# Earlier first exponentials of a softmax attention, fed by their own quad's maxima, and unread products among the row maxima

## The reference, cut to what matters

```python
c_q = x @ W_dq;  Q = (c_q @ W_uq).reshape(Bx, Sx, 16, 8)
c_kv = x @ W_dkv
K = (c_kv @ W_uk).reshape(Bx, Sx, 16, 8)
V = (c_kv @ W_uv).reshape(Bx, Sx, 16, 8)
scores = jnp.einsum('bqhd,bkhd->bhqk', Q, K) / math.sqrt(8)
scores = jnp.where(causal, scores, -jnp.inf)
attn = jax.nn.softmax(scores, axis=-1)
out = jnp.einsum('bhqk,bkhd->bqhd', attn, V).reshape(Bx, Sx, 128)
return out @ W_o
```

## Time and profile before

| | |
|---|---|
| median of 3 runs | 1094.41 us (1093.99 to 1094.48) |
| the profiled execution's own time | 1092.62 us |
| its span, first to last instruction | 1090.8 us |
| TensorE busy | 963.0 us, 88% |
| VectorE busy | 756.0 us, 69% |
| mean granted TensorE clock | 0.923 of 2.4 GHz |

### The profile page before, as it was taken

The page is one execution under the profiler, slowest core; times in us unless marked ns, Lnnn a source line. Parts: engine busy times, 40 slices in busy tenths (PEclk is TensorE's granted clock), DMA queues, the critical chain, the costliest instruction groups (busy, mean ns, idle before and its releaser), DMA issues.

```text
span 1090.8 us, 17904 instructions
## 1 busy us (share of the span) xinstructions
PE 963.0 (88%) x6094; PEld 463.7 (43%) x6094; DVE 756.0 (69%) x1559; ACT 560.3 (51%) x618; POOL 345.7 (32%) x740
## 2 busy tenths in 40 slices
PE   5799999999999775899738889999999989999996
PEld 3222223322224443699624323333333335666664
DVE  7689999999987687244366967877778225654456
ACT  4479889888987322122233025555555764422232
POOL 2163445245345300578802013333333431000000
PEclk9599999999999998899965559999999989999999
DMA  6201101110200402277444221122211300001001
GB/s 198 97 1 45 45 1 44 43 32 11 82 1 15 123 29 53 66 177 188 77 125 159 89 89 45 46 90 90 56 34 44 104 2 1 1 15 44 1 1 39
DMA packets 49836, 65.44 MB, mean 60 GB/s; under 512 B 7800, under 2 KB 37848, under 8 KB 46296
## 3 DMA queue, kind: packets, MB, share of 16 engines
q1 hardware_dynamic: 44144, 60.21, 18.0%
q0 software_dynamic: 5632, 4.46, 2.8%
HBM read 51.74 MB, written 12.91 MB: 59 GB/s over the span
## 4 chain that ended last, share of the span: by engine, by line
PE 63%; DVE 23%; issue 7%; ACT 4%; POOL 1%; DMA 1%; DVEq 0%; SPq 0%; ACTq 0%
PE acc_ps L766 10%; PE causal_ps L1215 10%; PE acc_ps L1090 6%; DVE mx L517 6%; PE tail_ps L1036 5%; PE tail_ps L1230 5%; PE causal_ps L1073 4%; DVE R L1566 4%; PE causal_ps L728 3%; DVE tails L1572 3%; PE causal_ps L964 3%; PE tail_ps L964 2%; PE acc_ps L974 2%; PE causal_ps L739 2%; ACT EX L1433 2%
## 5 line engine op out<-in xcount | busy, mean ns | idle before, releaser
L1433 ACT ACTIVATE EX<-causal_ps 128x1024 f32<-128x1024 f32 (+1 forms) x160 | 147.2, 939 | 160.7 <-PE causal_ps L1073 159.6
L517 DVE TENSOR_REDUCE mx<-tail_ps 128x1 f32<-128x512 f32 x266 | 157.8, 633 | 41.4 <-PE tail_ps L1039 22.7
L1307 ACT ACTIVATE R<-R 128x2048 f32<-128x2048 f32 (+1 forms) x80 | 134.7, 1736 | 0.5 <-DVE R L1566 0.5
L1215 PE MATMUL causal_ps<-XT,w 128*128 128x512 f32 x256 | 115.7, 594 | 1.0 <-DVE hid_f L1991 1.0
L1073 PE MATMUL causal_ps<-QE,KE 75*128 75x512 bf16 (+3 forms) x384 | 104.3, 343 | 10.5 <-ACT EX L1433 5.3
L1036 PE MATMUL tail_ps<-KM,QM 72*128 72x512 bf16 (+1 forms) x320 | 105.4, 357 | 8.7 <-DVE mx L517 3.0
L1566 DVE TENSOR_SCALAR R<-causal_ps 128x1024 f32<-128x1024 f32 (+1 forms) x88 | 94.0, 1070 | 14.9 <-PE causal_ps L728 13.8
L2215 POOL TENSOR_TENSOR pacer<-eps_ln 128x1 f32<-128x1 f32 x160 | 31.3, 195 | 230.3 <-ACT EX L1433 229.5
L1314 ACT ACTIVATE R<-R 128x1792 f32<-128x1792 f32 (+4 forms) x80 | 100.4, 1267 | 0.0
L1572 DVE TENSOR_REDUCE tails<-causal_ps 128x1 f32<-128x768 f32 (+4 forms) x96 | 92.9, 967 | 10.6 <-PE causal_ps L739 10.0
L1474 ACT ACTIVATE act_f<-causal_ps 128x512 f32<-128x512 f32 x64 | 38.1, 597 | 119.2 <-PE causal_ps L1215 119.2
(11 more groups left out here) (297 smaller groups left out, 1600.9 us busy)
## 6 DMA issues: line engine op xcount, KB each, us to landing
QS<-q_parts SPq DMA_DIRECT2D x8, 576.0 KB
KS<-k_parts SPq DMA_DIRECT2D x24, 192.0 KB
QM<-q_parts SPq DMA_DIRECT2D x8, 576.0 KB
KM<-k_parts SPq DMA_DIRECT2D x24, 192.0 KB
QE<-q_parts SPq DMA_DIRECT2D x8, 576.0 KB
KE<-k_parts SPq DMA_DIRECT2D x24, 192.0 KB
wg<-in_wg_t SPq DMA_DIRECT2D x16, 256.0 KB
wu<-in_wu_t SPq DMA_DIRECT2D x16, 256.0 KB
```

The lines of the kernel that those rows point to most:

```text
L517: return reduce(mx[:, par, hh, o0:o0 + step * (cnt - 1) + 1:step], scores[:, 0:cnt * w].rearrange("p (c w) -> p c w", w=w), AX.X, op, **how)
L1215: mm = pe.matmul(banks[2 * m + o], w[:, k, m * P:(m + 1) * P], XT[:, n * BANK:(n + 1) * BANK], start=True, stop=True)
L1307: act.activation(R4[:, rp, h0:h0 + 2, 0:width], R1[:, rp, h0:h0 + 2, 0:width], ACT.Square).then_inc(squared, 1)
L1433: act.activation(EX[:, rp, hh, 0:width], causal_ps[hh % 2][:, 0:width], ACT.Exp, scale=float(D) ** -0.5).then_inc(exp_done, 1)
```

## The change

Three things, all at the start of the second attention.

1. Quad 0's maxima are turned and cut as soon as quad 0's 40 jobs are reduced (`parts_of_max(0, 0)` at i = 39 instead of 47; on TensorE `turn_max(0)` behind the fifth job of quad 1). SyncE has quad 0's exponential stack loaded before that, and stores and reloads the maxima's parts at once. The exponentials of quad 0 begin when 14 of quad 1's maxima are done (`BEFORE_EXP`), not all 40.
2. Quad 1's other 26 maxima jobs go among stages 0 and 1 of quad 0's exponentials (`second_job`, in the two banks of `tail_ps`); quad 2's 40 follow in stages 2 to 4, 14, 13 and 13. Quad 1's maxima are turned in stage 2.
3. From job 26 of quad 0 to job 13 of quad 1, a `hold(1, 7)` stands ahead of each of the 28 jobs: one unread product of 128 rows into the second half of `acc_ps`.

```diff
-FIRST_TURN = 8
+FIRST_TURN = 5
+BEFORE_EXP = 14
+SECOND_AT = [BEFORE_EXP, BEFORE_EXP + 13, len(MAX), len(MAX), len(MAX), len(MAX)]
+THIRD_AT = [0, 0, 0, 14, 27, len(MAX)]
...
-            for par in range(2):
-                sp.wait_ge(first_full, len(MAX) * (par + 1))
-                load_max(2 + par, par)
-                store_max(par)
-                load_exp(par, par)
+            load_exp_stack(0, 0)
+            store_max(0)
+            load_exp_rows(0, 0)
+            load_max(2, 0)
+            load_exp_stack(1, 1)
+            sp.wait_ge(first_full, len(MAX) * 2)
+            load_max(3, 1)
+            store_max(1)
+            load_exp_rows(1, 1)
...
+            def second_job(n):
+
+                pe.wait_ge(first_max, len(MAX) + n - 1)
+                row_scores(tail_ps[:, n % 2 * BANK:(n % 2 + 1) * BANK], 1, n).then_inc(first_full, 1)
+
...
-                for i in range(len(MAX)):
+                for i in range(BEFORE_EXP if g else len(MAX)):
+                    if (g, i) >= (0, 26):
+                        hold(1, 7)
                     first_job(g, i)
-
-            pe.wait_ge(first_max, 2 * len(MAX))
+            for n in range(2):
+                second_job(BEFORE_EXP + n)
+            pe.wait_ge(first_max, len(MAX) + BEFORE_EXP)
...
+            def first_exp_quad():
+
+                pe.wait_ge(exp_in[0], 16 * (STACK_DMAS + 1))
+                for s in range(NS):
+                    jobs = [cut for hh in range(HQ) for cut in exp_scores(0, 0, s, hh)]
+                    if s:
+                        jobs = jobs[:2] + spread(jobs[2:], exp_sums(0, 0, s - 1))
+                    second = [(0, lambda n=n: second_job(n)) for n in range(max(SECOND_AT[s], BEFORE_EXP + 2), SECOND_AT[s + 1])]
+                    third = [(0, lambda n=n: max_job(2, 0, n)) for n in range(THIRD_AT[s], THIRD_AT[s + 1])]
+                    if s == 2:
+                        run_all(jobs[:3])
+                        turn_max(1)
+                        pe.wait_ge(max_in[0], 16 * STACK_DMAS * 2)
+                        jobs = jobs[3:]
+                    run_all(among(jobs, second + third))
...
-                maxima(g, n, banks[i % 6], dve.tensor_reduce, ALU.max, negate=True).then_inc(first_max, 1)
-                if i == len(MAX) + FIRST_TURN - 1:
+                bank = 4 + n % 2 if i >= len(MAX) + BEFORE_EXP else i % 6
+                maxima(g, n, banks[bank], dve.tensor_reduce, ALU.max, negate=True).then_inc(first_max, 1)
+                if i == len(MAX) - 1:
                     parts_of_max(0, 0)
```

More of the change, by code:

```diff
@@ L631, in store_max, with load_exp_stack, load_exp_rows @@
                 sp.dma_start(one_of_rows(m_rows, g).rearrange("r (h t) -> h r t", t=P), mparts[:, :, :]).then_inc(m_out, 16)
-            def load_exp(g, par):
+            def load_exp_stack(g, par):
+                load_stack(QE[:, par, :, :], KE[:, par, :, :], g, exp_in[par])
+            def load_exp_rows(g, par):
                 sp.wait_ge(m_out, 16 * (g + 1))
-                load_stack(QE[:, par, :, :], KE[:, par, :, :], g, exp_in[par])
                 sp.dma_start(QE[ROWS:MROWS, par, :, :].rearrange("r h t -> r (h t)"), one_of_rows(m_rows, g)
@@ L656, in _ @@
                     sp.wait_ge(exp_summed, NS * (2 * j + 1 + par))
-                    load_exp(2 * j + 2 + par, par)
+                    load_exp_stack(2 * j + 2 + par, par)
+                    load_exp_rows(2 * j + 2 + par, par)
             for par in range(2):
@@ L660, in _ @@
                 sp.wait_ge(exp_summed, NS * (NQ - 3 + par))
-                load_exp(NQ - 2 + par, par)
+                load_exp_stack(NQ - 2 + par, par)
+                load_exp_rows(NQ - 2 + par, par)
             sp.wait_ge(max_full, len(MAX) * (NQ - 2))
@@ L1139, in project_first, with exp_quad @@
                     times_w(1, n, 5)
-            def exp_quad(g, k, par, with_max, first=False, turn_maxima=True, beside=None):
+            def first_exp_quad():
[12 more added lines that the diff above has]
+                    run_all(among(jobs, second + third))
+            def exp_quad(g, k, par, with_max, turn_maxima=True, beside=None):
                 pe.wait_ge(exp_in[par], 16 * (STACK_DMAS + 1) * (k + 1))
@@ L1147, in exp_quad @@
                     run_all(exp_scores(g, par, 0, hh))
-                if first:
-                    turn_max(1, acc_ps)
-                    pe.wait_ge(m_sb, 2)
-                else:
-                    if turn_maxima:
-                        turn_max(g + 1)
-                    run_all(exp_sums(g - 1, 1 - par, NS - 1))
-                run_all(exp_scores(g, par, 0, 2))
-                if not first:
-                    pe.wait_ge(m_sb, g + 2 if turn_maxima else NQ)
-                    at_least(pe, e_normed, g - 1)
-                    if not turn_maxima:
-                        pe.wait_ge(yt_sb, CH + CH // B)
-                        pe.wait_ge(z_sb, CH + CH // B)
-                    turn_exp(g - 1)
+                if turn_maxima:
+                    turn_max(g + 1)
+                run_all(exp_sums(g - 1, 1 - par, NS - 1))
+                run_all(exp_scores(g, par, 0, 2))
+                pe.wait_ge(m_sb, g + 2 if turn_maxima else NQ)
+                at_least(pe, e_normed, g - 1)
+                if not turn_maxima:
+                    pe.wait_ge(yt_sb, CH + CH // B)
+                    pe.wait_ge(z_sb, CH + CH // B)
+                turn_exp(g - 1)
                 run_all(exp_scores(g, par, 0, 3))
@@ L1170, in exp_quad @@
                             among(jobs, beside[s]) if beside else jobs)
-            exp_quad(0, 0, 0, True, first=True)
+            first_exp_quad()
             exp_quad(1, 0, 1, True)
@@ L1886, in parts_of_max @@
                     dve.wait_ge(m_out, 16 * g)
-                src = (acc_ps if isinstance(g, int) and g < 2 else tail_ps)[0:HQ * KT, 0:P]
+                src = (acc_ps if isinstance(g, int) and g == 0 else tail_ps)[0:HQ * KT, 0:P]
                 def then(n, ins):
```

## The result

The changed kernel takes 1100.35 us (median of 4 runs, 1098.69 to 1101.83) against 1094.2 of the kernel before on the same chip: a ratio of 1.006 with an interval of 1.0047 to 1.0072 (here and below the ratio is estimated from all runs of both kernels, so it isn't quite the quotient of the two medians). It is slower by 6 us; the forecast was 7 us faster. The profiled execution took 1101.83 us.

The account below looks back on a forecast made before the run. VectorE's maxima were taken to bound the changed stretch: +2.3 - 4.1 - 5.5 = -7.3 us, taken as 7.0 off 1094.41, gives 1087.4 us; range for 8 in 10, 1084.2 to 1093.6.

Parts of the forecast that it names:

- the clock staying at 1.00 from 620 to 640: Sign to look for in the changed trace: TensorE's clock stays full there; a fall would be Case B.
- quad 1's other 26 maxima: Stages 0 and 1: 26 maxima at 0.604 us plus 1.05, 16.8 us, ending at 636.9; costs 2.3 us.
- quad 2's 40 maxima in three stages, all warm: Stages 2 to 4 at full clock: 27.85 us, ending at 667.6; gain 5.5 us (33.4 to 27.9).
- Case B: Rival: the clock rises but falls again in stage 0 for 12 to 18 us; about -1.5 us, 1093; chance 0.25.
- The unread products: 28 products ahead of maxima jobs of quads 0 and 1: raise the clock within 8 us, cost 0.
- C: Rival: unread products never raise the clock, exponentials begin 4.0 us late; +5 us, 1099.5; chance 0.13.
- Quad 1's 14th maximum: After the earlier turn it still ends at 620.1 us; no gain there.
- SyncE's path: Quad 0's maxima parts, stored and reloaded from about 614.4, leave 5.7 us until 620.1, so the loading is hidden.
- the turn: Quad 1's turn, moved to stage 2: 2.9 us in place of 7.0, gain 4.1 us.
- the forecast's 667.6: Time at which quad 2's last maximum was to end, in place of 675.04.
- The worked sum: Sum of the start's terms: +2.3 - 4.1 - 5.5 = -7.3 us, of which 7.0 was taken.
- D: Rival: clock full, but TensorE's order keeps VectorE waiting at 0.72 us a maximum; -4.3 us, 1090.1; chance 0.17.

Follow-up runs that it names:

- e10: Changed kernel with quad 2's 40 jobs split 4, 4 and 32 over stages 2, 3 and 4 instead of 14, 13, 13; 1103.43 us, ratio 1.0079.
- e9: Changed kernel plus only seven unread products behind quad 1's turn in stage 2; 1099.47 us, ratio 1.0027.
- e7: Changed kernel, but all 80 maxima ahead of the exponentials, quad 1's turn in stage 0, unread products ahead of 54 jobs; 1090.33 us, ratio 0.9975.
- e1: Changed kernel plus 16 unread products: four ahead of quad 1's job 14, one ahead of job 15 and each second_job of stage 0; 1088.98 us, ratio 0.9978.
- e8: Changed kernel plus 11 unread products, one ahead of each of jobs 16 to 26 in stage 0, none ahead of 14 and 15; 1097.27 us, ratio 1.0033.
- e5: e1 plus seven unread products behind quad 1's turn in stage 2; 1086.8 us, ratio 0.9933.
- e6: Changed kernel plus five unread products, four ahead of quad 1's job 14 and one ahead of job 15, none in stage 0; 1100.12 us, ratio 1.0052.
- e2: Changed kernel without its 28 unread products; 1097.69 us, ratio 1.0078.
- e4: Kernel before, in its own order, with an unread product ahead of each first job from quad 0's 27th on; 1090.06 us, ratio 1.0004.
- e3: Changed kernel with its 28 unread products 72 rows high instead of 128; 1102.95 us, ratio 1.012.
- e11: e5 plus three unread products in each later quad, ahead of the turn of the exponentials' sums; 1083.09 us, ratio 0.9923.

## Why the prediction was wrong

**The step that failed** is "the clock staying at 1.00 from 620 to 640", on which the terms "quad 1's other 26 maxima" and "quad 2's 40 maxima in three stages, all warm" both rest. It fell at 625.3. The 26 took 56.1 - 32.3 = 23.8 us instead of 16.8, the 40 took 35.5 instead of 27.85: 14.7 us, which turn -7.3 into +7.4, near the +8.0 measured. Case B had named this fall and its place, stage 0, and backed it with a fall from another place (896 to 902 in the earlier trace rows). It got 0.25, and my argument against it, that later quads have such stretches too, forgot that their stage 0 has the sums of the quad before it, and the first quad's has none. That this is the whole difference is argued, not shown. The rows were also of another kind than stage 0's: ahead of the fall at 899.3 TensorE did products of 128 rows and 8 columns.

```profile
897.23 1.85 PE L862 MATMUL tail_ps<-gate,XT 128*128 128x8 f32 x16
```

They showed that the clock can be lost without a gap, not that 72-row products lose it.

**B's size was wrong too.** I took the fall to last "as before, until the sums raise it: 12 to 18 us". It lasted 47.8. e10 shows that the sums raise it at +64.9 where few jobs stand between them, and e9 that seven products behind the turn do so at +61.7. In the changed kernel neither holds: its stages have 13 or 14 low jobs each, and TensorE is idle for 1.58 us at the turn. So the moved work helps to keep down the clock that its forecast pace needs. e7, without second-kind jobs in them, was cold for 10.2 us only. Why the same order is cold for 6.8 us in e1 and 20.5 in e8 stays open. The price per us was near: after against e5, the same order with the clock held, is 94.5 - 80.6 = 13.9 us for 47.8 us, 0.29 a us, where I had 4.5 / 12 = 0.375.

**What I had not seen**: the wait of 2.19 us ahead of job 14. It stands in no trace of before, but the order of the banks would have told it: the first jobs with two banks reuse those of the last two with six. e8's profile shows it losing the clock in its own right; e6 that filling it alone doesn't help.

**What was right, by e5, where the clock holds:**
- The unread products raise the clock in 5 us (8 forecast) and cost nearly nothing: at the 54th maximum 0.6 us (e2) to 1.0 (e4), at the 120th nothing. C, that they never raise it, is what 72 rows would have done (e3); there the first exponential is 7 us late, more than the 4.0 I had as a bound, and the whole is 1.012 where I had +5 us, 1.005.
- Quad 1's 14th maximum at +32.2 (forecast 620.1 - 588.6 = 31.5), with `m_sb` and SyncE's path hidden.
- The 26 maxima 17.9 us (16.8), the turn 2.7 (2.9), the 40 maxima 27.8 (27.85). The 120th maximum at +80.6 where the forecast's 667.6 is +79.0. Another 1.1 comes back behind it, in the span, as 1.0 does in the changed kernel (414.6 and 414.7 against 415.7).
- The sum: 495.3 against 502.2 us from the first maximum to the end of the span, -6.9; ratio 0.9933, which is -7.3 us of 1093.5. The worked sum was -7.3.

D, the pace of 0.72, is seen nowhere at the full clock: e5's 40 maxima go at 27.8 / 40 = 0.695.

**Where the time of the change went**, against the kernel before: the first exponential comes 12.8 us earlier, but the 80th maximum 10.1 us later, since TensorE at the low clock is the bound; 4.1 are gained at the turn (2.9 for 7.0); quad 2's 40 maxima take 35.5 us instead of 33.5. 10.1 - 4.1 + 2.0 = 8.0.

**What stays open.** Whether the same falls in later quads make the four long runs of the kernel before: e7's profile fits this, but no profile of such a run of before exists, and e5, with the later waits bare, had no long run in eleven. And why the second low stretch of the last stages lasts 13.7 us in e9 (900.4 to 914.1) and 3.4 in the kernel before (899.3 to 902.7), with the same code there; the first lasts 3.4 us in e9 and 6.8 before.

## What to carry to other kernels

Before work is moved to a place where its cost is worked out at the full clock, look at what TensorE does there: if it is products of few rows, or a short wait between such, the clock is part of the change's price, and "as long as before" is not a bound on a fall, because the moved work itself may help to keep it down. Ask of every weak place (the first use of a smaller set of banks, a turn, a stage without high products) whether it alone is enough to lose the clock: here three were, and with one or none of them covered the kernel was no faster than before, with the wait and stage 0 covered 0.9978 (no other pair was run), with all three 0.9933. Unread products of full height in a free bank, put where TensorE waits anyway, cost VectorE's chain 1.0 us at most, and they are all that differs between the changed kernel (1.006) and e5 (0.9933).

## What the runs showed of the hardware

- The height of the products made the difference between a clock that rises and one that doesn't: 85.38 of 88.00 us busy, mostly with 72 rows, left it at 0.50 (e3); one 128-row product a job raised it 5 us after the first (after, e4, e5). Nor did high products always hold it: in the kernel before it fell at 899.3, behind sixteen products of 128 rows and 8 columns that took 1.85 us.
- The clock was lost without a long gap: 2.5 us behind a wait of 2.19 us with low products after it (after), within such a wait (e8), 0.4 us behind one of 2.42 us among 128-row products (e4), and in three quads of one execution behind a wait of 1.05 us that eleven other profiles bear (e7).
- A rise is worth nothing where another engine is the bound: e4, with the full clock for most of its maxima, has its 120th maximum to the tenth where the kernel before has it.
- How long it stays lost isn't set by the order alone: 6.8 us in e1's profile, 20.5 in e8's, with the same stages.
- The kernels that hold the clock through the first quads are even, 3.1 us from the shortest to the longest run (e5, e11). Of those that lose it some spread, e1 by 9, e7, e8 and e9 by 12 to 13 us, but not all: e6's ten runs lie within 2.5.
